# A fused attention, GRU and block-attention kernel: second attention's inverses in two tiles, residual begun with three outputs, recurrent weights split in the last batch, first batch by halves of the heads

## The chip, the cores and the metric

One core of a Trainium2 chip runs the whole program. The metric is device time in microseconds (us), the median of several executions. Beside it there is one profiled execution, from which every row below is taken. PE is TensorE (its weight loads are PEld), DVE is VectorE, ACT is ScalarE, POOL is GpSimd, and SP is the engine that issues most transfers.

## The reference

```python
x = x + L0(x, mask=cond)   # batch 8, 256 channels, 512 positions: 16 heads of 16, masked softmax attention
x = x + L1(x, emb=cond)    # 256 tokens of 512: FiLM scale/shift = cond @ W_emb + b_emb, RMS norm,
                           # qkv, RMS norm of each head, 16 heads of 32, softmax; returns o + o @ W_out
x = x + L2(cond, x)        # GRU over 256 steps: gi = x @ W_ih + b_ih, gh = h @ W_hh + b_hh
x = x + L3(x)              # 8 blocks of 32 tokens: keys, softmax over blocks, projection, layer norm
```

## The kernel before

The program has three blocks in sequence: `attention` (L0 and L1 of all 8 batches), `recurrence` (the GRU) and `block_attention`. Between two blocks all engines meet.

**Attention.** Each engine walks the same written-out lists of steps, so the lists are the order of the work. For batch b there are `ATTEND[b]` (32 score units of the first attention, `st`, and their weighting, `pv`) and `BESIDE[b]`. `BESIDE[b]` finishes the second attention of batch e = b-1 (`score1`, `weigh1`, `inv1`, `out1`, `res`, `xT`), computes queries and keys of batch b (`tokens`, `xnT`, `qk`), and puts between them the 32 `max` steps, in which PE computes scores of batch b+1 and DVE reduces them to maxima (L1034). `BESIDE[7]` has no maxima, since there is no ninth batch. `ALONE0` comes first: the 32 maxima of batch 0 with nothing beside them, `neg`, and `row`, a small transpose whose result ACT sends by a transfer into `q_rep`; the first scores wait for that. `LONE` comes last: the second attention of batch 7 alone.

**The end of the second attention of a batch.** Heads go in G = 4 groups. `weigh1` g writes weighted values and sums of group g into bank g % 2 of `bank_pair_D`. `inv1` g on ACT makes the inverse of the sums with Ln (L900) and Exp (L902) in one tile `inv_sum`. `out1` g on DVE multiplies it onto the values and writes quarter g of `oT` (L1068). `res` oc on PE (L737, L740), for each of four output chunks, adds the tokens by two products with the identity and then four products of `W_out` with the four quarters of `oT`. `xT` on DVE (L1027) ends the batch.

**The start.** PE computes the queries of batch 0 (L546, `bank_pair_A`), the keys (`bank_pair_B`), the values (L558) and the eight FiLM chunks of four products each (L782). ACT and DVE split queries and keys into high and low halves of f16 (`q_hi`, `q_lo`, `k_hi`, `k_lo` in `parts`); SP stores each of the four to DRAM (L464), waits for all, and loads them back spread over partitions for the four groups of heads (`load_rep`, L476). The maxima of a group wait for its load.

**The recurrence.** Its prologue splits `W_hh` and makes the input products of the first 32 steps, 12 chunks m of 16 products (L1233) in two banks in turn, which ACT moves out (L1373). `W_hh` is loaded (L1217) and then split by ACT (L1389) ahead of the moves of chunks 3 to 6, and by DVE (L1421). The last four chunks have transposes of `Wk` and `Wo` ahead of them (L1301). L1317 opens the banks of the first step, and 256 steps follow.

```python
                if g >= 1:
                    act.wait_ge(oT_ok, e * G + g)
                nc.scalar.activation(inv_sum[:, :], pD[:, g % 2, N:2 * N], ACT.Ln).then_inc(log1_ok, 1)
```

Of the kernel before, what the change touches and what calls it, by code (L numbers as in the profile page):

```python
# [10 lines left out]
ALU = mybir.AluOpType  # L11
# [3 lines left out]
P = 128  # L15
# [6 lines left out]
G = H // 4  # L22
# [18 lines left out]
def build(nc, x, cond, Wq0, Wk0, Wv0, b0, W_emb, b_emb, g_norm, W_qkv, g_q, g_k, W_out,  # L41
          W_ih, W_hh, b_ih, b_hh, rms_w, Wk3, Wo3, gamma, beta, out):
    top = ExitStack()
    with top:
# [6 lines left out]
        def scratch(name, shape, dt):  # L51
# [16 lines left out]
        w_ih = (w_in, sem("w_ih_ld"), sem("w_ih_hi"), sem("w_ih_lo"))  # L68

        attention(nc, sem, sb, x, cond, Wq0, Wk0, Wv0, b0, W_emb, b_emb, g_norm, W_qkv, g_q, g_k, W_out,  # L70
                  mask_rows, parts0, parts1, pA, pB, pC, pD, xT, ident, condT, rep, W_ih, w_ih)
# [7 lines left out]
        recurrence(nc, sem, sb, W_ih, W_hh, b_ih, b_hh, Wk3, Wo3, pA, pB, pC, pD, xT, ident, condT, rep, w_ih, woT, block_sums,  # L79
# [8 lines left out]

def key_weights(rep):

    start = DC * 3 * D
    return as_f32(rep)[:, start:start + DC * D].rearrange("p (c n) -> p c n", c=DC)


def attention(nc, sem, sb, x, cond, Wq0, Wk0, Wv0, b0, W_emb, b_emb, g_norm, W_qkv, g_q, g_k, W_out,
              mask_rows, parts0, parts1, pA, pB, pC, pD, xT, ident, condT, rep, W_ih, w_ih):

    w_in, w_ih_ld, w_ih_hi, w_ih_lo = w_ih
    with ExitStack() as ctx:
# [40 lines left out]

        hi1 = parts[:, 0:2, :, :].rearrange("p a c (e n) -> p a (c e) n", e=2)
# [6 lines left out]
        inv_sum = t("inv_sum", [P, N])  # L148
# [22 lines left out]
        with ExitStack() as prep:  # L171
# [66 lines left out]
            def _(pe):  # L238
# [9 lines left out]
                for c in range(DC):  # L248
# [16 lines left out]
                             "exp1_ok", "pv1_ps", "inv1_ok", "log1_ok", "oT_ok", "res_ps", "xT_ok"))  # L265
        ticked, log0_ok, x1_last, ld_rep1_end = (sem(n) for n in ("ticked", "log0_ok", "x1_last", "ld_rep1_end"))
# [49 lines left out]
        def finish_order(with_max):  # L316
# [85 lines left out]
        def lone_order():  # L402
# [23 lines left out]
        ALONE0 = [("max", u) for u in range(U0)] + [("neg", 0), ("row", 0)]  # L426
# [6 lines left out]
        def _(sp):  # L433
# [31 lines left out]

            def load_rep(b, g):
# [6 lines left out]
                sp.wait_ge(st_parts, b * 64 + 64)  # L473
# [33 lines left out]
            for b in range(B):  # L507
# [21 lines left out]
                spread1(b)  # L529

        @block.tensor
        def _(pe):
            def project_qk(b, which, n):
# [14 lines left out]
                if n == NC * NC - 1:  # L548
                    last.then_inc((q_ps, k_ps)[which], 1)
# [181 lines left out]
            def residual(e, oc):  # L731

                if oc == 0:
                    pe.wait_ge(oT_ok, e * G + G)
                o = pD[:, oc // 2, (oc % 2) * N:(oc % 2) * N + N]
                for tc in range(NC):
                    nc.tensor.matmul(o[:, tc * P:tc * P + P], x1[e % 2][:, tc, oc * P:oc * P + P], ident[:, :],  # L737
                                     start=(oc % 2 == 0 and tc == 0), stop=False, skip_group_check=True)
                for c in range(DC):
                    last = nc.tensor.matmul(o, wout[:, c, oc * P:oc * P + P], oT[:, c, :], start=False, stop=(c == DC - 1),  # L740
                                            skip_group_check=True)
# [3 lines left out]
            def steps(order, b, e):  # L745

                for kind, n in order:
# [10 lines left out]
                    elif kind == "max":  # L758
                        max_scores(b + 1, n)
                    elif kind == "row":  # L760
# [18 lines left out]
            def film_chunk(m):  # L779

                for k in range(DC):
# [4 lines left out]
            for which in range(2):  # L786
                for n in range(NC * NC):
                    project_qk(0, which, n)
# [3 lines left out]
            pe.wait_ge(c_emb, 32)  # L792
            for m in range(2 * DC):
                film_chunk(m)
# [10 lines left out]
        def _(act):  # L805
            def q_parts(b):

                act.wait_ge(q_ps, b + 1)
# [50 lines left out]
            def qk_chunk(e, m):  # L859
# [9 lines left out]
                def hi_part(m):  # L869
                    if m == 0 and e + 1 < B:  # L870
                        act.wait_ge(st_parts, e * 64 + 128)
# [964 lines left out]
```

## Time and profile before

| | us |
|---|---|
| median of 3 runs (1967.75 to 1971.98) | 1971.07 |
| the profiled execution | 1970.45 |
| span of its trace | 1968.5 |
| PE busy | 1854.3 (94%) |
| DVE busy | 1260.1 (64%) |
| ACT busy | 1090.5 (55%) |
| POOL busy | 378.4 (19%) |

In the rows further down a line of the timeline reads: start and duration in us, engine, source line, operation, output<-inputs, shape, the count of instructions merged, and in brackets the idle time ahead of it with what ended it. Ends of matmuls are modelled, and a full row of PE is not PE at its peak. PEclk is the granted clock of PE as a share of 2.4 GHz, so 0.50 is 1.2 GHz.

### The profile page before, as it was taken

The numbers are of one execution on the slowest core, as the hardware profiler recorded it, in microseconds if no ns is written. First come the engines' busy times: TensorE is split into PE (matmuls) and PEld (weight loads), VectorE is DVE, ScalarE is ACT, GpSimd is POOL, SyncE is SP. The second block draws the span as 40 slices with busy tenths as digits, with TensorE's granted clock in tenths as the row PEclk, the third lists the DMA queues.
The fourth block names the chain that finished last, engine by engine and source line by source line (L and its number), as shares of the span: only waits on it lengthen the run. The fifth ranks groups of instructions, "written<-read, shape, count | busy, mean of one in ns | idle before, by whom it ended". The sixth has DMA issues, their size and how long they took to land. (4 is left out here: it accounts for less than half of the span.)

```text
span 1968.5 us, 87065 instructions
## 1 busy us (share of the span) xinstructions
PE 1854.3 (94%) x33006; PEld 1408.4 (72%) x33006; DVE 1260.1 (64%) x5543; ACT 1090.5 (55%) x4105; POOL 378.4 (19%) x1398
## 2 busy tenths in 40 slices
PE   7877999999999999999978999999999999999996
PEld 4234465565646556464747999999999999999995
DVE  5545474746647475573244777777777777777767
ACT  0342737547373664737534665656565656666555
POOL 3000000000000000000001434343434343433335
PEclk7688999999999999999988999999999999999997
DMA  5221313233041322203223000000000000000002
GB/s 177 87 82 44 94 31 101 68 81 88 19 114 37 87 81 65 88 2 81 87 47 114 0 1 0 0 0 0 0 0 0 0 0 0 0 0 1 0 0 86
DMA packets 103525, 86.73 MB, mean 44 GB/s; under 512 B 15616, under 2 KB 90496, under 8 KB 103440
## 3 DMA queue, kind: packets, MB, share of 16 engines
q1 hardware_dynamic: 102416, 85.43, 15.3%
q8 instruction: 57, 0.93, 0.2%
q0 software_dynamic: 384, 0.01, 0.0%
q14 instruction: 28, 0.23, 0.0%
q10 hardware_dynamic: 640, 0.13, 0.0%
HBM read 60.20 MB, written 21.00 MB: 41 GB/s over the span
## 5 line engine op out<-in xcount | busy, mean ns | idle before, releaser
L1246 PE MATMUL bank_pair_A<-moving,rep 128*128 128x16 f16 x8192 | 317.9, 169 | 2.5 <-ACT bank_pair_C L1337 1.4
L1246 PE MATMUL bank_pair_B<-moving,rep 128*128 128x16 f16 x8192 | 315.4, 169 | 0.0
L1246 PE MATMUL bank_pair_C<-moving,rep 128*128 128x16 f16 x8192 | 315.4, 169 | 0.0
L1246 PEld LDWEIGHTS bank_pair_A<-moving,rep 128*128 128x128 f16 x8192 | 274.4, 96 | 14.3 <-issue 4.1
L1346 ACT ACTIVATE r_gate<-r_pre 128x16 f32<-128x16 f32 x512 | 110.5, 216 | 285.6 <-DVE r_pre L1437 285.6
L1246 PEld LDWEIGHTS bank_pair_B<-moving,rep 128*128 128x128 f16 x8192 | 258.9, 96 | 0.0
L1246 PEld LDWEIGHTS bank_pair_C<-moving,rep 128*128 128x128 f16 x8192 | 258.8, 96 | 0.0
L1233 PE MATMUL bank_pair_D<-x_part,w_in 128*128 128x256 f16 x1536 | 198.8, 275 | 7.0 <-ACT gi_rz L1373 4.4
L1034 DVE TENSOR_REDUCE head_max<-bank_pair_A 128x2 f32<-128x1024 f32 x128 | 155.9, 1218 | 56.6 <-PE bank_pair_A L579 56.4
L1437 DVE TENSOR_REDUCE r_pre<-bank_pair_A 128x16 f32<-128x32 f32 x512 | 97.9, 191 | 136.2 <-PE bank_pair_A L1246 136.2
L1128 POOL TENSOR_TENSOR x<-x,w_in 128x512 f32<-128x512 f32 x8 | 10.2, 1271 | 896.3 <-DMA w_in<-w_in 896.3
L1034 DVE TENSOR_REDUCE head_max<-bank_pair_B 128x2 f32<-128x1024 f32 x128 | 155.6, 1216 | 21.3 <-PE bank_pair_B L579 20.8
L1233 PEld LDWEIGHTS bank_pair_D<-x_part,w_in 128*128 (+1 forms) x1536 | 138.3, 98 | 23.4 <-ACT gi_rz L1373 4.7
L836 ACT ACTIVATE probs<-bank_pair_A 128x1024 f32<-128x1024 f32 x128 | 130.9, 1023 | 43.4 <-PE bank_pair_A L598 43.1
L1527 POOL COPY n_terms<-gi_n 128x32 f32 (+1 forms) x257 | 53.8, 209 | 487.5 <-DVE moving L1488 437.6
L610 PE MATMUL bank_pair_C<-probs,w_in 128*32 128x512 f32 x1024 | 136.9, 607 | 0.2 <-ACT probs L836 0.2
L836 ACT ACTIVATE probs<-bank_pair_B 128x1024 f32<-128x1024 f32 x128 | 131.1, 1024 | 7.7 <-PE bank_pair_B L598 7.7
L598 PEld LDWEIGHTS bank_pair_A<-rep 128*128 128x128 f16 x512 | 40.6, 98 | 115.9 <-ACT probs L836 95.5
L1346 ACT ACTIVATE z_gate<-z_pre 128x16 f32<-128x16 f32 x512 | 110.6, 216 | 20.2 <-DVE z_pre L1441 9.1
L1446 DVE TENSOR_TENSOR n_terms<-bank_pair_B,r_gate 128x32 f32<-128x32 f32 x512 | 97.7, 191 | 28.7
L879 ACT ACTIVATE sq<-bank_pair_C 128x256 f32<-128x256 f32 x48 | 18.4, 383 | 169.4 <-PE bank_pair_C L640 169.4
L1346 ACT ACTIVATE cand<-n_pre 128x16 f32<-128x16 f32 x512 | 107.0, 209 | 0.0
(262 smaller groups left out, 3764.0 us busy)
## 6 DMA issues: line engine op xcount, KB each, us to landing
rep<-parts SPq DMA_DIRECT2D x256, 64.0 KB
parts<-parts SPq DMA_DIRECT2D x48, 256.0 KB, 2.1
q_rep<-parts SPq DMA_DIRECT2D x32, 256.0 KB, 5.0
k_rep<-parts SPq DMA_DIRECT2D x64, 128.0 KB, 2.9
w_in<-in_x_dram SPq DMA_DIRECT2D x8, 512.0 KB, 3.9
x<-in_x_dram SPq DMA_DIRECT2D x8, 512.0 KB, 4.0
w_in<-w_in SPq DMA_DIRECT2D x128, 32.0 KB, 2.0
parts<-parts SPq DMA_DIRECT2D x32, 128.0 KB, 2.6
```

Source lines behind the costliest of these rows:

```text
L598: last = nc.tensor.matmul(pair[u % 2][:, j // 2, (j % 2) * N:(j % 2) * N + N], k_rep[:, h, kc * P:kc * P + P], q_rep[:, h, queries], start ...
L610: last = nc.tensor.matmul(pC[32 * j:32 * j + 32, g % 2, :], v_aug[:, kc, 4 * g + j, :], probs[w % 2][:, j, :], start=(kc == 0), stop=(kc = ...
L836: nc.scalar.activation(probs[u // 2 % 2][:, :, u % 2 * N:u % 2 * N + N], pair[u % 2][:, :, :].rearrange("p a (b t) -> p (a b) t", b=2), AC ...
L879: nc.scalar.activation(sq[m % 2][:, :], qk_bank[m % 3][:, 0:N], ACT.Square).then_inc(sq_ok, 1)
L1034: nc.vector.tensor_reduce(head_max[:, 2 * n:2 * n + 2], pair[n % 2][:, :, :], AX.X, ALU.max).then_inc(s_max, 1)
L1128: nc.gpsimd.tensor_tensor(x1[b % 2][:, c, :], x1[b % 2][:, c, :], y[:, c, :], ALU.add).then_inc(x1_ok, 1)
L1233: last = nc.tensor.matmul(bank, w_in[w][:, k, bass.ts(m, P)], x_part[:, part, k, :, :].rearrange("p b t -> p (b t)"), start=(k == 0 and w ...
L1246: last = nc.tensor.matmul(ps[part][:, o:o + 2 * B], w[:, k, (first + c) * P:(first + c) * P + P], moving[j % 2][:, k, :, :].rearrange("p s ...
L1346: nc.scalar.activation(dst[:, SLICE[part], :], src[:, SLICE[part], :], func, scale=1.0 / GS).then_inc(done, 1)
L1437: nc.vector.tensor_reduce(r_pre[:, SLICE[part], :], halves(pR[part]), AX.X, ALU.add).then_inc(r_sum, 1)
L1446: nc.vector.tensor_tensor(n_terms[:, SLICE[part], 0:2, :], pN[part].rearrange("p (c s b) -> p c s b", s=2, b=B), r_gate[:, SLICE[part], :] ...
L1527: nc.gpsimd.tensor_copy(n_terms[:, :, 2, :], gi_n[:, bass.ds(step, 1), :, :].rearrange("p o c b -> p (o c) b")).then_inc(n_in, 1)
```

## The change

It has four parts, all in `attention` and in the prologue of `recurrence`.

1. `inv_sum` becomes two tiles (those of `head_rstd`), so `inv1` of a group waits for the `out1` of two groups before. In `BESIDE` the `out1` of the third group moves ahead of `weigh1` of the fourth, and the `out1` of the fourth ahead of the second of two maxima.
2. `residual` starts once three quarters of `oT` are there: for chunks 0 and 1 it adds tokens and three products each, waits for the fourth quarter, then adds the fourth products of both. Chunks 2 and 3 are as before.
3. `W_hh` is loaded into the tile of `W_qkv` after the last use of it, and split in `LONE`, by ACT after its last inverse and by DVE between the last `out1` and `xT`. The load and split are gone from the recurrence.
4. In batch 0 queries and keys are computed, split and stored by halves of the heads: groups 0 and 1 are loaded after the first half is stored, groups 2 and 3 after the second. On DVE the addition of the bias to `q_rep` (L1079) goes between the halves. Of the eight FiLM chunks three stay ahead of the maxima, one goes ahead of `row`, four follow it.

```diff
@@ finish_order (BESIDE)
             yield "inv1", G - 2
+            yield "out1", G - 2
             yield "weigh1", G - 1
-            yield from maxes(1)
-            yield "out1", G - 2
             yield "inv1", G - 1
             yield from maxes(1)
             yield "out1", G - 1
+            yield from maxes(1)
             yield "tokens", 0
...
@@ lone_order and alone_order
             yield "out1", G - 1
+            yield "w_hh", 0
...
+            for m in range(3):
+                yield "film", m
+            for u in range(U0):
+                yield "max", u
+            yield "neg", 0
+            yield "film", 3
+            yield "row", 0
+            for m in range(4, 2 * DC):
+                yield "film", m
...
@@ SP
-            store_parts(0, 0)
-            store_parts(0, 1)
-            for g in range(G):
-                load_rep(0, g)
+            for c in range(2):
+                store_first(c)
+                for g in range(2 * c, 2 * c + 2):
+                    load_rep(0, g)
...
                 spread1(b)
+            sp.wait_ge(v1_ps, B)
+            sp.dma_start(wqkv[:, :, :], W_hh.rearrange("(c p) n -> p c n", p=P)).then_inc(w_ld, 16)
...
@@ residual on PE
                 if oc == 0:
+                    pe.wait_ge(oT_ok, e * G + (G - 1))
+                if oc < 2:
+                    tokens_part(oc)
+                    weights_part(oc, range(DC - 1))
+                if oc == 1:
                     pe.wait_ge(oT_ok, e * G + G)
+                    weights_part(0, (DC - 1,))
+                    weights_part(1, (DC - 1,))
+                if oc >= 2:
+                    tokens_part(oc)
+                    last = weights_part(oc, range(DC))
...
@@ inverse1 on ACT
-                if g >= 1:
-                    act.wait_ge(oT_ok, e * G + g)
-                nc.scalar.activation(inv_sum[:, :], pD[:, g % 2, N:2 * N], ACT.Ln).then_inc(log1_ok, 1)
+                if g >= 2:
+                    act.wait_ge(oT_ok, e * G + (g - 1))
+                nc.scalar.activation(inv_sum[g % 2][:, :], pD[:, g % 2, N:2 * N], ACT.Ln).then_inc(log1_ok, 1)
...
+            def split_w_hh():
+                act.wait_ge(w_ld, 16)
+                act.wait_ge(w_ih_lo, DC)
+                for k in range(DC):
+                    nc.scalar.activation(w_part[0][:, k, :], wqkv[:, k, :], ACT.Copy, scale=WS).then_inc(w_hi, 1)
...
@@ batch 0 on ACT
-            q_parts(0)
-            k_part(0)
+            for c in range(NC):
+                act.wait_ge(q_ps, c + 1)
+                nc.scalar.activation(q_hi[:, c, :], pA[:, c, :], ACT.Copy, scale=QS).then_inc((half_hi, q_hi_ok)[c], 1)
...
+                nc.scalar.activation(k_hi[:, c, :], kf[:, c, :], ACT.Copy).then_inc((half_hi, k_hi_ok)[c], 1)
...
@@ batch 0 on DVE
+            dve.wait_ge(ld_mask, 16)
+            for c in range(NC):
...
+                if c == 0:
+                    dve.wait_ge(c_b, 3)
+                    nc.vector.tensor_scalar(q_rep[64:67, :, :], q_rep[64:67, :, :], brow[64:67, 0:1], None, ALU.add).then_inc(c_b, 1)
...
@@ recurrence
-            sp.dma_start(staged, W_hh.rearrange("(c p) n -> p c n", p=P)).then_inc(w_ld, 16)
...
-                if W_HH_FROM <= m < W_HH_FROM + DC:
-                    k = m - W_HH_FROM
-                    if k == 0:
-                        act.wait_ge(w_ld, 16)
-                    nc.scalar.activation(w_part[0][:, k, :], staged[:, k, :], ACT.Copy, scale=WS).then_inc(w_hi, 1)
                 evacuate(0, m, pG[m % 2], m >= RZ)
```

The first place is PE between the last maximum of batch 0 and the first scores. `bank_pair_D<-condT,probs` are the FiLM products, `bank_pair_A<-ident,head_max` is `row`. Before:

```order
L579 MATMUL bank_pair_B<-rep 128x512 x2
L585 MATMUL bank_pair_A<-ident,head_max 64x128
L598 MATMUL bank_pair_A<-rep 128x256 x4
L598 MATMUL bank_pair_B<-rep 128x256 x4
L546 MATMUL bank_pair_D<-w_in,W0T 128x512
```

The same place with the change:

```order
L611 MATMUL bank_pair_B<-rep 128x512 x2
L835 MATMUL bank_pair_D<-condT,probs 128x8 x4
L617 MATMUL bank_pair_A<-ident,head_max 64x128
L835 MATMUL bank_pair_D<-condT,probs 128x8 x16
L630 MATMUL bank_pair_A<-rep 128x256 x4
L630 MATMUL bank_pair_B<-rep 128x256 x4
```

Five FiLM chunks, 20 products, now stand around `row`, 16 of them between it and the first scores; 12 of the 32 remain ahead of the maxima.

The second place is the end of the second attention of a batch with maxima, on DVE. The rows with `oT` are `out1`, those with `xnT` are the normed tokens. Before, from the `out1` of the second group:

```order
L1068 TENSOR_TENSOR oT<-bank_pair_D,inv_sum 128x256
L1034 TENSOR_REDUCE head_max<-bank_pair_B 128x2
L1034 TENSOR_REDUCE head_max<-bank_pair_A 128x2
L1068 TENSOR_TENSOR oT<-bank_pair_D,inv_sum 128x256
L1034 TENSOR_REDUCE head_max<-bank_pair_B 128x2
L1068 TENSOR_TENSOR oT<-bank_pair_D,inv_sum 128x256
L1001 TENSOR_SCALAR xnT<-bank_pair_C,film_scale,film_shift 128x256 x4
```

With the change:

```order
L1135 TENSOR_TENSOR oT<-bank_pair_D,head_rstd 128x256
L1099 TENSOR_REDUCE head_max<-bank_pair_B 128x2
L1135 TENSOR_TENSOR oT<-bank_pair_D,head_rstd 128x256
L1099 TENSOR_REDUCE head_max<-bank_pair_A 128x2
L1135 TENSOR_TENSOR oT<-bank_pair_D,head_rstd 128x256
L1099 TENSOR_REDUCE head_max<-bank_pair_B 128x2
L1066 TENSOR_SCALAR xnT<-bank_pair_C,film_scale,film_shift 128x256 x4
```

Each of the last two `out1` stands one maximum earlier.

The third place is ACT from the last inverse of the last batch to the moves of the recurrence's chunks (`gi_rz`). Before:

```order
L902 ACTIVATE inv_sum<-inv_sum 128x256
L99 UNCONDITIONAL_BRANCH
L1322 UNCONDITIONAL_BRANCH
L1326 ACTIVATE x_part<-xT 128x256 x4
L1327 ACT_TABLE_LOAD
L1373 ACTIVATE gi_rz<-bank_pair_D,bias_in 128x8x32 x3
L1389 ACTIVATE rep<-gi_rz 128x1536
L1373 ACTIVATE gi_rz<-bank_pair_D,bias_in 128x8x32
```

With the change:

```order
L953 ACTIVATE head_rstd<-head_rstd 128x256
L992 ACTIVATE rep<-wqkv 128x1536 x4
L107 UNCONDITIONAL_BRANCH
L1402 UNCONDITIONAL_BRANCH
L1406 ACTIVATE x_part<-xT 128x256 x4
L1407 ACT_TABLE_LOAD
L1453 ACTIVATE gi_rz<-bank_pair_D,bias_in 128x8x32 x8
```

The four splits of 1536 columns leave the moves and stand ahead of the boundary between the blocks.

## Rows read from the trace of the kernel before

**Rows 1.** Timeline of batch 0 up to the first maximum

```profile
15.05 0.19 PEld L546 LDWEIGHTS bank_pair_A<-w_in,W0T 128*128 128x128 f32 x1 [0.46 <-issue]
...
16.96 1.02 ACT L811 ACTIVATE parts<-bank_pair_A 128x1024 f16<-128x1024 f32 x1 [14.93 <-PE bank_pair_A L546]
...
20.47 1.29 DVE L962 SCALAR_TENSOR_TENSOR kf<-bank_pair_B,w_in 128x512 f32<-128x512 f32 x2 [1.23 <-PE bank_pair_B L546]
...
22.95 1.23 DVE L969 TENSOR_TENSOR parts<-kf,parts 128x1024 f16<-128x1024 f32 x1 [1.19 <-ACT parts L815]
...
23.65 9.12 PE L782 MATMUL bank_pair_D<-condT,probs 128*128 128x8 f32 x64
...
26.34 4.70 SPq L476 DMA_DIRECT2D rep<-parts  x8
...
33.85 1.22 DVE L1034 TENSOR_REDUCE head_max<-bank_pair_A 128x2 f32<-128x1024 f32 x1 [9.68 <-PE bank_pair_A L579]
```

**Rows 2.** Timeline from the last maximum of batch 0 to the first scores

```profile
70.49 1.22 DVE L1034 TENSOR_REDUCE head_max<-bank_pair_B 128x2 f32<-128x1024 f32 x1
...
72.00 0.69 PE L585 MATMUL bank_pair_A<-ident,head_max 128*64 128x128 f32 x2 [1.55 <-DVE head_max L1037]
...
75.25 1.01 PE L598 MATMUL bank_pair_A<-rep 128*128 128x256 f16 x4 [2.57 <-DMA rep<-max_row]
```

**Rows 3.** Windows: busy time (instructions) by engine, PEclk, DMA share, GB/s

```profile
26.00:29.00 3.00, 3.00 (x28) 3.00 (x27) 0.00 (x0) 0.00 (x0) 0.00 (x0) 0.94 0.13 37
29.00:32.80 3.80, 3.77 (x18) 3.70 (x19) 0.00 (x0) 0.00 (x0) 0.00 (x0) 0.50 0.45 134
...
79.00:80.00 1.00, 1.00 (x5) 0.69 (x3) 0.00 (x0) 0.29 (x1) 0.00 (x0) 0.58 0.00 0
```

**Rows 4.** Timeline of the end of a second attention, e = 0

```profile
269.80 0.42 ACT L902 ACTIVATE inv_sum<-inv_sum 128x256 f32<-128x256 f32 x1
...
271.62 1.23 DVE L1034 TENSOR_REDUCE head_max<-bank_pair_A 128x2 f32<-128x1024 f32 x1 [2.24 <-PE bank_pair_A L579]
...
272.76 0.41 DVE L1068 TENSOR_TENSOR oT<-bank_pair_D,inv_sum 128x256 f32<-128x256 f32 x1
...
273.27 0.38 ACT L900 ACTIVATE inv_sum<-bank_pair_D 128x256 f32<-128x256 f32 x1 [3.05 <-DVE oT L1068]
...
274.69 0.71 PE L737 MATMUL bank_pair_D<-ident,x 128*128 128x128 f32 x4 [1.80 <-DVE oT L1068]
```

**Rows 5.** Waits of all attention from 85 us: total us, times, longest

```profile
PE bank_pair_D L737 <- DVE oT L1068: 12.6, 8, 1.8
```

**Rows 6.** Windows, the stage behind the residual of e = 0

```profile
286.00:312.00 26.00, 26.00 (x109) 18.72 (x108) 17.66 (x27) 13.02 (x33) 0.00 (x0) 1.00 0.30 63
```

**Rows 7.** Timeline of the last batch

```profile
984.99 5.59 ACT L939 ACTIVATE w_in<-rep 128x1536 f16<-128x1536 f32 x4
...
1004.28 6.75 DVE L1102 SCALAR_TENSOR_TENSOR w_in<-rep,w_in 128x1536 f16<-128x1536 f32 x4
...
1022.95 0.71 PE L737 MATMUL bank_pair_D<-ident,x 128*128 128x128 f32 x4 [1.41 <-DVE oT L1068]
...
1031.95 1.23 DVE L1027 TENSOR_TENSOR xT<-bank_pair_D,oT 128x1024 f32<-128x1024 f32 x1 [9.05 <-PE bank_pair_D L740]
```

**Rows 8.** Timeline of the recurrence's prologue

```profile
1034.50 10.56 PE L1233 MATMUL bank_pair_D<-x_part,w_in 128*128 128x256 f16 x80 [2.59 <-DVE x_part L1403]
...
1047.35 1.48 ACT L1389 ACTIVATE rep<-gi_rz 128x1536 f16<-128x1536 f32 x1 [5.05 <-DMA gi_rz<-in_L_cond_W_hh_dram]
...
1049.48 6.93 PE L1233 MATMUL bank_pair_D<-x_part,w_in 128*128 128x256 f16 x48 [4.42 <-ACT gi_rz L1373]
...
1056.25 1.04 PE L1301 MATMUL bank_pair_A<-ident,gi_rz 128*128 128x128 f32 x8
```

**Rows 9.** Windows of the prologue

```profile
1040.00:1045.00 5.00, 5.00 (x47) 4.29 (x44) 0.00 (x0) 1.26 (x2) 0.00 (x0) 1.00 1.02 422
```

**Rows 10.** A transfer of the prologue: KB, us from issue to landing

```profile
gi_rz<-in_L_cond_Wk_dram SPq DMA_DIRECT2D x1, 1024.0 KB, 14.3
```

More of the change, by code:

```diff
@@ L78, in build @@
         norm_from = (cond, rms_w, beta, gamma)
-        recurrence(nc, sem, sb, W_ih, W_hh, b_ih, b_hh, Wk3, Wo3, pA, pB, pC, pD, xT, ident, condT, rep, w_ih, woT, block_sums,
+        recurrence(nc, sem, sb, b_ih, b_hh, Wk3, Wo3, pA, pB, pC, pD, xT, ident, condT, rep, w_ih, w_hh, woT, block_sums,
                    norm, norm_from)
@@ L86, in as_f32, with halves_of_weights @@
     return rep[:, :, :, :].rearrange("p n h d -> p (n h d)").bitcast(F32)
+def halves_of_weights(rep):
+    words = rep[:, :, :, :].rearrange("p n h d -> p (n h d)")[:, 0:2 * DC * 3 * D].rearrange("p (s c n) -> p s c n", s=2, c=DC)
+    return [words[:, n, :, :] for n in range(2)]
 def key_weights(rep):
@@ L265, in attention @@
                              "exp1_ok", "pv1_ps", "inv1_ok", "log1_ok", "oT_ok", "res_ps", "xT_ok"))
+        half_hi, half_low = (sem("half_" + n) for n in ("hi", "low"))
         ticked, log0_ok, x1_last, ld_rep1_end = (sem(n) for n in ("ticked", "log0_ok", "x1_last", "ld_rep1_end"))
@@ L424, in lone_order, with alone_order @@
             yield "xT", 0
-        ALONE0 = [("max", u) for u in range(U0)] + [("neg", 0), ("row", 0)]
+        def alone_order():
+            for m in range(3):
[7 more added lines that the diff above has]
+                yield "film", m
+        ALONE0 = list(alone_order())
         ATTEND = [list(attend_order(b)) for b in range(B)]
@@ L731, in residual, with tokens_part, out_of, weights_part @@
             def residual(e, oc):
-                if oc == 0:
-                    pe.wait_ge(oT_ok, e * G + G)
[L735 to L741, printed above, removed]
+                def tokens_part(oc):
+                    for tc in range(NC):
+                        nc.tensor.matmul(out_of(oc)[:, tc * P:tc * P + P], x1[e % 2][:, tc, oc * P:oc * P + P], ident[:, :],
+                                         start=(oc % 2 == 0 and tc == 0), stop=False, skip_group_check=True)
+                def out_of(oc):
+                    return pD[:, oc // 2, (oc % 2) * N:(oc % 2) * N + N]
+                def weights_part(oc, chunks):
+                    for c in chunks:
+                        last = nc.tensor.matmul(out_of(oc), wout[:, c, oc * P:oc * P + P], oT[:, c, :], start=False, stop=(c == DC - 1),
+                                                skip_group_check=True)
+                    return last
+                if oc == 0:
+                    pe.wait_ge(oT_ok, e * G + (G - 1))
[3 more added lines that the diff above has]
+                if oc == 1:
+                    pe.wait_ge(oT_ok, e * G + G)
+                    weights_part(0, (DC - 1,))
[3 more added lines that the diff above has]
+                    last = weights_part(oc, range(DC))
                 if oc == DC - 1:
@@ L1097, in _, with split_w_hh @@
             nc.vector.tensor_scalar(gk[:, :], gk[:, :], QS * DH1 ** 0.5, None, ALU.mult).then_inc(c_gains, 1)
+            def split_w_hh():
+                for k in range(DC):
+                    dve.wait_ge(w_hi, k + 1)
+                    nc.vector.scalar_tensor_tensor(out=w_part[1][:, k, :], in0=wqkv[:, k, :], scalar=WS, in1=w_part[0][:, k, :],
+                                                   op0=ALU.mult, op1=ALU.subtract).then_inc(w_lo, 1)
             def split_w_ih():
@@ L1188, in recurrence @@
         RZ = 2 * DC
-        W_HH_FROM = 3
         def halves(ps):
```

81 lines of the change are left out of this document (50 added, 31 removed).

## Prediction

> **What bounds the kernel now.** I read the table of busy times first: TensorE (PE) is at 94% of the span, so the attention blocks and the recurrence are rows of PE work with gaps, and a gap that is closed shortens the program if PE stays busy after it. So I went through the waits of PE, then the timeline around each gap that the change touches, then the windows for the clock. The reader should see four things.
> First, the start. PE is idle or slow for 72 us. The split keys of batch 0 end on DVE at 22.95 + 1.23 = 24.18, the loads of group 0 go out from 26.34, and the first maximum is reduced at 33.85 [rows 1]. From there DVE alone sets the pace: 32 maxima from 33.85 to 70.49 + 1.22 = 71.71 [rows 1, 2], or 1.18 each.
> Second, PE waits for `out1` at the head of the residual: 12.6 us in 8 batches [rows 5], 1.80 in a batch with maxima [rows 4] and 1.41 in the last [rows 7]. Six such batches make 10.8, so batch e = 6 has 12.6 - 10.8 - 1.41 = 0.4.
> Third, after it PE is busy without a gap (26.00 of 26.00 us) [rows 6].
> Fourth, the recurrence's prologue. Five chunks of products end at 1034.50 + 10.56 = 1045.06, then PE stands 4.42 us, because the move of a bank is queued on ACT behind the split of `W_hh`, and that waited 5.05 us for its load; three more chunks then take 6.93, and the first transposes start at 1056.25 [rows 8].
>
> **Part 4, the halves.** Moved, not added: the same bytes in eight stores of half the size, with a second wait for stores. The fifth weight load of the queries starts at 15.05 [rows 1]; the four ahead of it are the first half of the heads for both chunks of channels, so ACT can take `q_hi` of the first half at 15.1. Half of 1.02 is 0.5, with a fixed share some 0.6: 15.7. DVE needs 1.29 / 2 = 0.65: `q_lo` to 16.4. The second products end near 16.9, since the first full bank was read at 16.96 [rows 1]. `kf` 0.65 to 17.6, `k_hi` on ACT 0.6 to 18.2, `k_lo` 0.65 to 18.9. The whole keys end at 24.18 now, 5.3 later. Behind that the chain is unchanged: 2.16 from `k_lo` to the loads (24.18 to 26.34) puts them at 21.1, and the first maxima at most 5.3 earlier. In PE nothing is in the way: 24 of the 64 FiLM instructions remain ahead, 2.6 us at 0.107 each (28 in 3.00) [rows 3], which end at 23.65 + 2.6 = 26.3, before the loads land. The bias (L1079) now stands between the halves on DVE; the second half of the stores is issued behind 16 loads on SP near 30, and groups 2 and 3 land by about 41, while their maxima are due 16 times 1.18 behind 28.5, at 47. So the second half costs nothing; the cover is 6 us. Value: -5.3.
> **Part 4, the FiLM chunks.** The 40 instructions taken from the front return at the end of the maxima, where the clock is half. FiLM ran there at 0.107 each at full clock and 0.211 at half (18 in 3.80) [rows 3]. Chunk 3, 8 instructions, takes 1.7 in a gap of 1.55 ahead of `row` [rows 2]: +0.15. The 32 behind `row` take 6.75 us at half clock. `row` ends near 72.6, so they end at 79.5 in the old times, where the scores began at 75.25 after a transfer [rows 2]. That transfer hides 2.6 us of them. What is queued behind them is the first scores, and for those ACT waits. So +4.1. Start in all: -5.3 + 0.15 + 4.1 = -1.1.
> The clock decides that term. It read 1.00 after dense products, fell from full to half while PE was busy with FiLM products alone (0.94 on average in 26 to 29, 0.50 in 29 to 32.8) [rows 3], and came back in 79 to 80, some 4.3 us after the scores began at 75.25 [rows 2, 3]. I therefore take FiLM as work that doesn't raise it. By the Trainium skill (TensorE: Matmul & The Clock Gate, Part 1) activity of PE releases the throttle; by that rule PE, busy from chunk 3 on, would have its full clock before the scores. This trace speaks against counting FiLM as such activity, but shows only the fall, not the rise; it is the second rival.
>
> **Parts 1 and 2, six batches with maxima.** Now: Exp of group 2 ends at 270.22, DVE is idle 2.24 us before a maximum at 271.62, `out1` of group 2 comes behind it at 272.76, the Ln of group 3 at 273.27 waited 3.05 for that, and PE starts the residual at 274.69 [rows 4]. With the change `out1` of group 2 falls into DVE's idle time at 270.3. Ln and Exp of group 3 need only PE's sums, which end ahead of the products of the maximum reduced at 271.62; with 0.38 + 0.42 they are done by 272.4. Its `out1` takes the old place at 272.76 and ends at 273.2. PE, free at 274.69 - 1.80 = 272.89, needs three quarters only, so it goes on at once, and has 3.5 us of products before it needs the fourth (a chunk of the residual is a quarter of 1031.95 - 1022.95 [rows 7], 2.25, and all but the fourth products of two chunks come first). The gap goes whole: 1.80 each, -10.8. DVE's second maximum keeps its place, and the maxima inside the residual stay a step ahead of PE. After it PE shows no idle time in 26 us [rows 6], and what it releases (loads, `qk`, `xT`) hangs on it and shifts along.
> **Batch e = 6 and the last.** 0.4 and 1.41 [rows 5, 7]: PE fills them with products of three quarters. In the last batch DVE now has four splits of `W_hh` ahead of `xT`. On ACT they take 5.59 / 4 = 1.40 each and can start at 1022.45, on DVE 6.75 / 4 = 1.69 each [rows 7]: from 1023.9 to 1030.7. The residual would end at 1031.95 - 1.41 = 1030.5, so `xT` loses 0.1 to 0.2. Together -0.4 - 1.3 = -1.7. The load of 3 MB is issued behind the last spread of keys near 996 and has 26 us to land; in the prologue today the same load ends ACT's wait at 1047.35 [rows 8], issued at the block's start near 1034.5, so under 13 us. Nothing stands behind it on SP.
>
> **Part 3, the prologue.** Without split and wait the moves keep ahead of PE, as they did in the first five chunks, which ran without a gap [rows 8]. At full clock a product takes 5.00 / 47 = 0.106 [rows 9], a chunk of 16 takes 1.70. The last three before the transposes then end at 1045.0 + 5.1 = 1050.1, not 1056.25: -6.1. Some of that is clock, since PE also came back slow after the gap. The transposes need `Wk` and `Wo`. `Wk` took 14.3 us with 3 MB ahead of it [rows 10]; now it is issued where those were, at the start of the block near 1034.5, and even 14.3 would give 1049, before PE asks. `Wo`, of the same size, follows it. Value: -6.0.
>
> **The sum.** -1.1 - 10.8 - 1.7 - 6.0 = -19.6. The profiled execution took 1970.45, its span being 1968.5, so 1950.8; the median is 0.6 above it, so 1951.4. I forecast 1951. What follows, 256 steps and the block attention, is unchanged.
>
> **Rivals.**
> 1. The halves bring nothing: DVE's order or the landing of the smaller stores holds the first maxima where they are. For it: 2.16 us from `k_lo` to the loads is a wait for landing, paid twice now. Against: PE's 5.3 are on the chain. Then the start costs +4.2 instead of -1.1, time 1956.5. Chance 0.12.
> 2. FiLM counts as activity. The clock rises about 4.3 us after chunk 3 starts, at 74.8; by then some 10 of the 32 instructions have run, the other 22 take 2.4, and the scores start at 77.2 at full clock. Today they start at 75.25 and lose 2.2 at half clock, which is 77.4. The +4.1 vanishes: 1947. Chance 0.15.
> 3. The freed PE time is not passed on in the six batches: DVE, with its maxima, or a transfer ends the next wait. For it: DVE is 18 of 26 us busy there. Against: no idle time of PE after the residual [rows 6]. Half lost gives 1956.5, all lost 1962. Chance 0.1.
> 4. Slower. The half clock after the maxima persists into the first `ATTEND`, because PE meets it with long FiLM work of low load instead of a pause. Each microsecond of dense work at half clock costs 0.5, so it decides from 39 us more at half clock on; with 60, 1981. For it: PE stayed at half clock through the maxima. Against: the same scores raised it in 4.3 us [rows 2, 3]. Chance 0.02.
> The forecast itself (1949 to 1954) has 0.58; the rest are small mixtures around it.
>
> **Range and chances.** It must reach rival 2 below and rivals 1 and 3 in part above: 1946 to 1958. A measurement of this kernel tells 0.2%, 4 us. Only rival 4 and an unforeseen wait of that size end above 1967: faster 0.95, same 0.03, slower 0.02.
>
> **What would show it.** After: the first maximum on DVE near 28.5; FiLM products behind `row` for 6 to 7 us at half clock, and the first scores 1 us earlier than now; no wait of PE at the head of any residual; `xT` of the last batch right behind four splits on DVE; no gap of PE in the prologue, and the first transposes of `Wk` some 20 us before 1056.25. I am wrong if scores start before 72 or after 76, if PE's idle time at the residual returns a few steps later, or if the last maxima of keys wait longer for their load.

## The result, and the profile after

The changed kernel took 1946.35 us (median of 4 runs, 1945.18 to 1949.10) beside 1969.41 for the kernel before: a ratio of 0.9879, 95% interval 0.9862 to 0.9895. The same kernel in another set of runs gave 0.9869 (0.9854 to 0.9885). The mean of the two ratios, 0.9874, is 24.8 us less than the 1970.4 of before; the forecast's sum was 19.6. Wherever a gain or loss in us is given below, it is a difference of such ratios times 1970.4. The profiled execution took 1949.1 us and is the slowest of its four, its span 1947.1.

The page's table of busy times of the changed kernel:

```profile
PE 1852.5 (95%) x33006; PEld 1410.3 (72%) x33006; DVE 1262.5 (65%) x5545; ACT 1092.0 (56%) x4107; POOL 379.4 (19%) x1398
```

PE's busy time is 1.8 us below that of before, the span 21.4: the time came out of PE's idle time.

**The start.** Timeline of the changed kernel up to the first maximum, the place of [rows 1]:

```profile
11.54 1.95 PE L578 MATMUL bank_pair_A<-w_in,W0T 128*128 128x512 f32 x4 [1.82 <-PEq L179]
...
13.53 0.60 ACT L1002 ACTIVATE parts<-bank_pair_A 128x512 f16<-128x512 f32 x1 [11.49 <-PE bank_pair_A L578]
...
15.13 0.69 DVE L1148 SCALAR_TENSOR_TENSOR parts<-bank_pair_A,parts 128x512 f16<-128x512 f32 x1 [3.07 <-DMA w_in<-in_cond_dram]
...
17.11 0.69 DVE L1157 TENSOR_TENSOR parts<-kf,parts 128x512 f16<-128x512 f32 x1 [0.69 <-ACT parts L1007]
...
19.54 3.62 SPq L506 DMA_DIRECT2D rep<-parts  x8
...
21.93 2.74 PE L835 MATMUL bank_pair_D<-condT,probs 128*128 128x8 f32 x24
...
26.05 0.60 PE L611 MATMUL bank_pair_A<-rep 96*128 96x512 f16 x2 [1.38 <-DMA rep<-parts]
...
26.69 1.23 DVE L1099 TENSOR_REDUCE head_max<-bank_pair_A 128x2 f32<-128x1024 f32 x1 [3.73 <-PE bank_pair_A L611]
```

`q_hi` of the first half starts at 13.53. `q_lo` could follow at 14.13, but DVE waited for the load of the mask until 15.13, a wait that the forecast doesn't have. `k_lo` ends at 17.80, the loads go out at 19.54 and the first maximum is reduced at 26.69 instead of 33.85. The forecast said 28.5; experiment 9 shows why this execution was earlier still. PE now waits 1.38 us for the load, where it came from FiLM without a pause before.

From the last maxima to the first scores, the place of [rows 2], and two windows of the clock, one behind the first maxima and one behind the first scores (PEclk is the third number from the end):

```profile
63.08 1.71 PE L835 MATMUL bank_pair_D<-condT,probs 128*128 128x8 f32 x8
...
64.59 0.20 DVE L1102 TENSOR_SCALAR head_max<-head_max 128x64 f32<-128x64 f32 x1
64.84 0.69 PE L617 MATMUL bank_pair_A<-ident,head_max 128*64 128x128 f32 x2
65.45 7.00 PE L835 MATMUL bank_pair_D<-condT,probs 128*128 128x8 f32 x32
...
72.30 1.01 PE L630 MATMUL bank_pair_A<-rep 128*128 128x256 f16 x4
```

```profile
27.00:30.00 3.00, 2.13 (x5) 0.26 (x4) 3.00 (x3) 0.00 (x0) 0.00 (x0) 0.50 0.72 232
78.00:79.00 1.00, 1.00 (x6) 0.59 (x5) 0.00 (x0) 0.22 (x1) 0.00 (x0) 0.98 0.08 16
```

The 32 instructions take 7.00 us, 0.219 each, which is the half clock throughout. From `row` to the scores it is 7.46 us, before 3.25 [rows 2]. The clock is at its full level from about 78, 5.7 us behind the first scores.

**The end of a second attention.** Timeline of the changed kernel, e = 0, the place of [rows 4]:

```profile
268.41 0.42 DVE L1135 TENSOR_TENSOR oT<-bank_pair_D,head_rstd 128x256 f32<-128x256 f32 x1 [0.86 <-ACT head_rstd L953]
...
269.27 0.38 ACT L951 ACTIVATE head_rstd<-bank_pair_D 128x256 f32<-128x256 f32 x1 [0.89 <-PE bank_pair_D L758]
...
270.01 1.04 PE L655 MATMUL bank_pair_C<-ident,xn 128*128 128x128 f32 x8
...
270.89 0.61 PE L767 MATMUL bank_pair_D<-ident,x 128*128 128x128 f32 x4
270.92 0.41 DVE L1135 TENSOR_TENSOR oT<-bank_pair_D,head_rstd 128x256 f32<-128x256 f32 x1
```

The residual follows the transposes of the tokens with no idle time, and the fourth `out1` ends at 271.33, while PE still works on three quarters. The first products take 0.61 us where they took 0.71 behind the wait [rows 4]. PE's waits from 200 to 1060 us (total, times, longest) have no line of the residual left, where there were 12.6 us [rows 5]; the two largest that are left there are these:

```profile
PE bank_pair_A L707 <- DMA k_rep<-parts: 7.9, 2, 6.2
PE bank_pair_D L715 <- DVE head_max L1132: 7.3, 8, 2.0
```

**The last batch and the prologue**, the places of [rows 7] and [rows 8]:

```profile
1006.02 5.59 ACT L992 ACTIVATE rep<-wqkv 128x1536 f16<-128x1536 f32 x4
...
1007.52 6.76 DVE L1180 SCALAR_TENSOR_TENSOR rep<-wqkv,rep 128x1536 f16<-128x1536 f32 x4 [0.95 <-ACT rep L992]
...
1014.20 1.22 DVE L1092 TENSOR_TENSOR xT<-bank_pair_D,oT 128x1024 f32<-128x1024 f32 x1
...
1016.74 15.77 PE L1313 MATMUL bank_pair_D<-x_part,w_in 128*128 128x256 f16 x128 [2.64 <-DVE x_part L1478]
...
1032.35 1.04 PE L1381 MATMUL bank_pair_A<-ident,gi_rz 128*128 128x128 f32 x8
```

The splits lie beside PE's residual and `xT` follows them at 1014.20. The eight chunks ahead of the transposes run through in 15.77 us without a gap; from their start to the transposes it is 15.61, before 21.75 [rows 8].

How far the changed kernel is ahead of before in the two profiled executions: first scores 2.95; first residual 3.81; start of the last batch's residual 17.81; prologue 17.76; transposes 23.90; end 21.4. The recurrence gives none of this back: from the transposes to the first products of the block attention (1032.35 to 1891.83, before 1056.25 to 1915.79) it is 859.5 us in both traces. The 2.5 us are given back in the block attention, which the change doesn't touch: 55.3 us from there to the end, before 52.7. Its length differs between traces (52.8 in experiments 10 and 11, 53.8 in 4 and 7, 55.2 in 9 and 12); what makes the difference stays open.

### The profile page after: what moved, and what is told of

It is laid out like the page before. It is cut to its first block and busy times, and to the rows that moved or that the text cites. A ratio compares the mean times of both kernels' runs of the same rounds, so it can differ in the third digit from the quotient of the medians.

```text
span 1947.1 us, 87066 instructions
## 1 busy us (share of the span) xinstructions
PE 1852.5 (95%) x33006; PEld 1410.3 (72%) x33006; DVE 1262.5 (65%) x5545; ACT 1092.0 (56%) x4107; POOL 379.4 (19%) x1398
## 5 line engine op out<-in xcount | busy, mean ns | idle before, releaser
L1212 POOL TENSOR_TENSOR x<-x,w_in 128x512 f32<-128x512 f32 x8 | 10.2, 1272 | 878.6 <-DMA w_in<-w_in 878.6
```

## The experiments

The ratios are to the kernel before, with 95% intervals. A part is undone when it alone is taken out of the changed kernel, and what that loses is read against 0.9874, the mean of the changed kernel's two ratios. A part is alone when nothing else of the change is made to the kernel before. The intervals are about 3 us to either side, so a loss of 1 or 2 us is not told from none.

**1. Part 4 undone** (halves and FiLM as before).

```diff
-            for m in range(3):
+            for m in range(8):
                 yield "film", m
...
-            for c in range(2):
-                store_first(c)
-                for g in range(2 * c, 2 * c + 2):
-                    load_rep(0, g)
+            store_parts(0, 0)
+            store_parts(0, 1)
+            for g in range(G):
+                load_rep(0, g)
```

> The changed kernel with batch 0 as it was: queries and keys split and stored whole, eight FiLM chunks ahead of the maxima. Theory A (the terms of the sum are right, and the 3 us more than forecast are where PE's clock happened to be low in single executions): the first scores start 1 to 3 us later than with the change, the loss of 1.8 seen in the profile's start being half clock (the full clock came at 9.8 us there and at 15.0 before); time 1.1 to 3 above the changed kernel, 1947.5 to 1949.5. Theory B (the start was worth 1.1 + 3.5): 4.6 above, 1951.

1947.93 us, 0.9881 (0.9865 to 0.9896): 1.4 us lost. That is theory A's size, though the interval doesn't exclude B's 4.6; experiment 7 narrows it.

**2. Part 3 undone** (`W_hh` loaded and split in the recurrence).

```diff
-            yield "w_hh", 0
...
+                if 3 <= m < 3 + DC:
+                    k = m - 3
+                    if k == 0:
+                        act.wait_ge(w_ld, 16)
+                    nc.scalar.activation(w_part[0][:, k, :], staged[:, k, :], ACT.Copy, scale=WS).then_inc(w_hi, 1)
                 evacuate(0, m, pG[m % 2], m >= RZ)
```

> The changed kernel with the load and split of W_hh back in the recurrence's prologue. Theory A: 6.0 of the prologue comes back, less 0.15 that xT loses behind the splits: 5.9 above the changed kernel, 1952.2. Theory B (the last batch pays for the load and the splits, as its longer stretch at half clock in the profile may say): 4 above or less, 1950.3, and the last batch of this run is faster than with the change.

1952.41 us, 0.9902 (0.9887 to 0.9916): 5.5 us lost, near A. From the prologue's first product to the transposes it is 20.84 us in its trace. B asked for a faster last batch. From the seventh residual to the eighth it takes 67.36 us here and 68.28 in the changed kernel, but with 10.2 us at half clock against 17.1; experiment 1, which has part 3 and also 10.2 us at half clock, takes 66.50. So the traces don't show that the load and the splits cost the last batch anything.

**3. Parts 1 and 2 undone.**

```diff
+            yield from maxes(1)
+            yield "out1", G - 2
             yield "inv1", G - 1
...
                 if oc == 0:
-                    pe.wait_ge(oT_ok, e * G + (G - 1))
...
+                    pe.wait_ge(oT_ok, e * G + G)
+                tokens_part(oc)
+                last = weights_part(oc, range(DC))
```

> The changed kernel with one tile of inverses, the old order of out1 and the old residual. Theory A: 10.8 + 0.4 + 1.4 = 12.6 above the changed kernel, 1959. Theory B (the gaps were worth more, since closing them also keeps the clock up or frees DVE): 15 to 16 above, 1962. PE waits again 12.6 us at the head of the residuals.

1960.75 us, 0.9944 (0.9928 to 0.9960): 13.8 us lost. A and B both lie in the interval; the time doesn't choose between them.

**4. Five FiLM chunks ahead, one before `row`, two behind.**

```diff
-            for m in range(3):
+            for m in range(5):
...
-            for m in range(4, 2 * DC):
+            for m in range(6, 2 * DC):
```

> The changed kernel with five FiLM chunks ahead of the maxima, one ahead of row and two behind it, instead of 3, 1 and 4. In the changed kernel's profile PE stands 1.38 us ahead of the first maximum, and a chunk takes 0.9 there at full clock and 1.75 behind row. Theory A: two more chunks ahead delay the first maximum by 0.4 us and take 3.5 from behind row, of which 0.1 is below the transfer: scores 3 us earlier, 1943.3. Rival: the maxima wait for more, or the clock falls during the five chunks (it fell at 26.85 in the changed kernel's profile): no gain, 1946 to 1947.

1944.13 us, 0.9867 (0.9850 to 0.9885). The direction is A's, but 1.4 us are not told apart by these intervals. In the trace the scores follow the last maximum's `neg` by 4.30 us, against 7.71 in the changed kernel.

**5. Part 1 alone undone** (the first hunk of 3, and one tile of inverses).

```diff
-        inv_sum = head_rstd
+        inv_sum = [head_rstd[0], head_rstd[0]]
...
-                if g >= 2:
-                    act.wait_ge(oT_ok, e * G + (g - 1))
+                if g >= 1:
+                    act.wait_ge(oT_ok, e * G + g)
```

> Only part 1 is undone (one tile of inverses, the old order of inv1, weigh1 and out1 of the last two groups); the residual still begins with three quarters. Theory A, the early residual carries the gain nearly alone: in the old order the third quarter was ready at 272.76 + 0.41 = 273.17 and PE was free at 272.89, so PE waits 0.3 us at the head of the residual in six batches, 1.8 us in all, and never for the fourth quarter, which is needed 3.5 us later. That gives 1948.2 us, a ratio to before of 0.989. Rival B, the two parts bring half of the 1.9 us each: 6 us are lost, 1952.5, ratio 0.991. Rival C, undoing part 1 costs nothing at all: 1946.4.

1951.98 us, 0.9901 (0.9884 to 0.9918): 5.3 us lost, so B by the time. The trace has the wait that A named, and nothing of B's half a gap. Waits of PE, and the residual's head in the timeline:

```profile
PE bank_pair_D L767 <- DVE oT L1135: 2.0, 6, 0.3
```

```profile
272.95 0.71 PE L767 MATMUL bank_pair_D<-ident,x 128*128 128x128 f32 x4 [0.34 <-DVE oT L1135]
```

But 0.34 of wait lengthened that batch's stretch from ACT's move of `row` to the residual by 0.50 (78.76 against 78.26). Up to the seventh residual the trace is 3.8 us longer than those of the kernels with both parts (the table further down: 0.50 and 669.87 against 666.61), which is twice A's 1.8. How far the 5.3 are more than that, the interval leaves open.

**6. Part 2 alone undone** (the second hunk of 3).

```diff
                 if oc == 0:
-                    pe.wait_ge(oT_ok, e * G + (G - 1))
+                    pe.wait_ge(oT_ok, e * G + G)
```

> Only part 2 is undone: the residual waits for all four quarters at its head; the two tiles of inverses and the moved out1 stay. Theory A: in the trace of the changed kernel PE is free for the residual at 270.78 and the fourth out1 ends at 270.92 + 0.41 = 271.33, so PE waits some 0.6 us in six batches, 3.4 us; to this come the 0.4 of the seventh batch and up to 1.4 of the last, where no maximum stood in the way before: 5 us lost, 1951.4, ratio 0.9908. Rival B, part 1 alone closes the gap: 1947 at most. Rival C, part 1 alone closes nothing because the out1 stays behind a maximum: 13 us lost, 1959.

1952.58 us, 0.9906 (0.9889 to 0.9922): 6.3 us lost, A. The waits:

```profile
PE bank_pair_D L767 <- DVE oT L1127: 3.8, 8, 1.4
```

Each part undone loses 5 to 6 us, both together 13.8 (experiment 3), so either alone brings more than half: each gives `oT` more time, and they overlap.

**7. Part 4 alone on before** (edits 2 and 3 together).

```diff
-            yield "w_hh", 0
...
-                    pe.wait_ge(oT_ok, e * G + (G - 1))
+                    pe.wait_ge(oT_ok, e * G + G)
```

> Part 4 alone on the kernel before; parts 1, 2 and 3 undone. The trace of the changed kernel has the first scores 2.95 us earlier than before, the row of batch 1 1.85 us earlier; with part 4 undone that row was 0.7 us earlier. Theory A, part 4 is worth 1 to 2 us in time: ratio to before 0.999 (0.998 to 1.0). Rival B, the forecast's other ends: halves bring nothing, +4 us, ratio 1.002; or 5.3 us gained without a cost of FiLM, ratio 0.997.

1969.61 us, 0.9993 (0.9984 to 1.0002): 1.4 us gained, 3.2 at most, and the interval just includes nothing. A. The row of the residual's wait is back at 12.6 us, 8 times.

**8. All FiLM chunks ahead, halves kept.**

```diff
-            for m in range(3):
+            for m in range(8):
                 yield "film", m
...
-            yield "film", 3
             yield "row", 0
-            for m in range(4, 2 * DC):
-                yield "film", m
```

> The changed kernel with all eight FiLM chunks ahead of the maxima, as before, and the halves of the heads kept. Theory A, halves and FiLM trade one against the other as forecast: 40 instructions at 0.107 delay the first maximum by 4.3 less the 1.4 us in which PE waited for the load, to 29.6, and the scores follow row and its transfer only, near 71.0 to 71.5 instead of 72.3. So 1 us faster than the changed kernel, ratio 0.9874. Rival B: FiLM ahead costs more, because the first products then run at half clock: ratio 0.9889, 2 us slower.

1948.11 us, 0.9871 (0.9855 to 0.9886): the same time as the changed kernel, and A's ratio. A's mechanism was wrong all the same: its first maximum at 29.6 came at 36.88. This trace is of an execution 5 us above the kernel's median (1953.24), whose clock rose only at 17.6. Timeline of this kernel, then two windows:

```profile
24.97 11.00 PE L834 MATMUL bank_pair_D<-condT,probs 128*128 128x8 f32 x64
...
36.88 1.23 DVE L1098 TENSOR_REDUCE head_max<-bank_pair_A 128x2 f32<-128x1024 f32 x1 [11.42 <-PE bank_pair_A L610]
```

```profile
25.00:27.80 2.80, 2.80 (x28) 2.80 (x26) 0.46 (x1) 1.02 (x1) 0.00 (x0) 1.00 0.43 139
28.00:35.80 7.80, 7.80 (x38) 7.80 (x38) 0.00 (x0) 0.00 (x0) 0.00 (x0) 0.50 0.44 136
```

The clock fell while PE ran FiLM alone: 28 instructions in 2.80 us, then 38 in 7.80. So the last chunks cost half clock ahead of the maxima as well as behind them, and with all of them ahead PE, not the load, sets the first maximum: 36.88, against 37.17 in experiment 11, which has no halves and the same late start. [rows 1] has it already: FiLM ends at 23.65 + 9.12 = 32.77, and in the same trace the products of the first maximum start at 32.81, without a wait for the load. So by the traces the halves move the first maximum only because FiLM is moved. The times can't show it: 0.9871 here and 0.9881 without the halves (experiment 1) are not told apart.

**9. The changed kernel again** (no edit).

> The changed kernel again, unedited, beside the three below on one chip. Its first ratio was 0.9879 (0.9862 to 0.9895), 23.8 us below before, 4.2 more than the forecast's sum of 19.6. Theory A, the sum was short in its sizes (a fit over the kernels run so far gives 2.3 for part 4, 15.7 for parts 1 and 2 and 7.4 for part 3, 25.4 in all): 0.987 to 0.988 again. Theory B, the sum was right and the first ratio a lucky draw: 0.990.

1947.86 us, 0.9869 (0.9854 to 0.9885): A, above the forecast's 19.6 again. Its start in the timeline:

```profile
11.64 3.41 PE L578 MATMUL bank_pair_A<-w_in,W0T 128*128 128x512 f32 x4 [1.82 <-PEq L179]
...
28.32 1.23 DVE L1099 TENSOR_REDUCE head_max<-bank_pair_A 128x2 f32<-128x1024 f32 x1 [4.35 <-PE bank_pair_A L611]
```

The same four instructions took 1.95 us in the first trace. The clock rose in the one case before 10 us and in the other at 14.6, as it did at 15.0 in the trace of before. With that, the loads go out at 21.07 and the first maximum is at 28.32, where 21.1 and 28.5 were forecast.

**10. Part 3 alone on before** (edits 1 and 3 together).

```diff
+                    pe.wait_ge(oT_ok, e * G + G)
+                tokens_part(oc)
+                last = weights_part(oc, range(DC))
...
+            store_parts(0, 0)
+            store_parts(0, 1)
```

> Part 3 alone on the kernel before: W_hh loaded and split in the last batch, everything else as before. Theory A, the forecast's size: the gap of 4.42 us and the slow products after it go, 6.0 less, ratio 0.9969. Theory B, it is worth more (9.7 us between the kernel with parts 3 and 4 and the one with part 4 alone; 7.4 in the fit): 0.9950 to 0.9962. Rival C, less (4.5 us between the kernel with part 3 undone and the changed one): 0.9977.

1964.77 us, 0.9961 (0.9946 to 0.9976): 7.7 us gained; B's size, A within the interval. The prologue's stretch is 14.69 us in its trace.

**11. Parts 1 and 2 alone on before** (edits 1 and 2 together).

```diff
-            yield "w_hh", 0
...
+            store_parts(0, 0)
+            store_parts(0, 1)
```

> Parts 1 and 2 alone on the kernel before. Theory A, the waits at the head of the residual are all that goes: 10.8 + 1.7 = 12.5 us, ratio 0.9937. Theory B, a gap costs more than PE's listed wait, since the first product after it takes 0.71 instead of 0.61 and its weight load is in the open; the traces show 2.0 a batch and 14.4 us up to the seventh residual: 15.7 us, ratio 0.9920. Rival C, part of it is given back where no other part helps: 10 us, 0.9949.

1955.80 us, 0.9913 (0.9899 to 0.9928): 17.1 us gained. B (15.7); A's 0.9937 is outside the interval.

**12. FiLM among the maxima.** Two chunks as eight single products, one behind each fourth maximum; one chunk before `row`, two behind.

```diff
             for u in range(U0):
                 yield "max", u
+                if u % 4 == 3:
+                    yield "film1", 3 * DC + u // 4
             yield "neg", 0
-            yield "film", 3
+            yield "film", 5
             yield "row", 0
-            for m in range(4, 2 * DC):
+            for m in range(6, 2 * DC):
```

> The changed kernel with two FiLM chunks, eight products, spread one product behind every fourth maximum of batch 0, one chunk ahead of row and two behind it instead of four. Theory: DVE paces the maxima at 1.18 us, and PE has about 0.15 us of slack in each (20.89 busy of 24.00), 0.6 in four, against 0.44 for a product of two instructions at half clock. So the maxima end as before, 16 instructions behind row end 3.5 us earlier, and the first scores start near 69.0 instead of 72.3: 1943.0, ratio 0.986. Rival: a product behind a maximum delays the next fill of a bank by its whole 0.44, and DVE with it: 8 times 0.44 minus the slack, up to 3.5 us later, which cancels the gain: 1946.4.

1941.65 us, 0.9855 (0.9839 to 0.9871): the fastest kernel here, 3.7 us below the mean of the changed one, though the intervals overlap. It is as much as was expected, 3.5. Timeline:

```profile
30.59 1.23 DVE L1108 TENSOR_REDUCE head_max<-bank_pair_A 128x2 f32<-128x1024 f32 x1
...
31.48 0.43 PE L843 MATMUL bank_pair_D<-condT,probs 128*128 128x8 f32 x2
31.73 1.22 DVE L1108 TENSOR_REDUCE head_max<-bank_pair_B 128x2 f32<-128x1024 f32 x1
...
66.13 0.19 DVE L1111 TENSOR_SCALAR head_max<-head_max 128x64 f32<-128x64 f32 x1
...
70.75 1.01 PE L632 MATMUL bank_pair_A<-rep 128*128 128x256 f16 x4
```

From the first maximum (28.24) to `neg` it is 37.89 us, in the changed kernel 26.69 to 64.59, 37.90: the products fit into PE's slack at no cost to DVE. The scores follow `neg` by 4.62 instead of 7.71. So the expected mechanism is in the trace; only that it shortens the time is not beyond the intervals.

**All together.** A least-squares fit of three terms to eight of the ratios (the changed kernel twice, each of the three parts undone, each alone), weighted by their intervals:

| | forecast | alone on before | undone | fit |
|---|---|---|---|---|
| part 4 | 1.1 | 1.4 | 1.4 | 1.8 +- 1.4 |
| parts 1 and 2 | 12.5 | 17.1 | 13.8 | 16.5 +- 1.7 |
| part 3 | 6.0 | 7.7 | 5.5 | 7.4 +- 1.8 |
| all | 19.6 | | 24.8 | 25.7 |

The +- come from the runs' intervals alone; kernels measured together share the runs of before, so they are rather too small. By the fit part 4 can't be told from nothing, and parts 1 and 2 together are 4 us above their forecast, more than twice their +-.

## Why the prediction was right and where it fell short

The direction and the mechanisms held and none of the four rivals took their place. The size was 5.2 us short, 19.6 for 24.8, and by the traces about 3 of it are in one term, the six batches.

**Bounds.** Right. PE's gaps that were closed shortened the program whole, and by more than their length.

**Halves, -5.3.** Right for an execution whose clock rises as late as before's: 33.85 to 28.32 is 5.5 (experiment 9). The loads go out at 21.07 there, for 21.1. In the first trace the early clock made it 19.54, although DVE waited for the mask. The cover of the second half held. Rival 1 is refuted with FiLM where the change puts it. With FiLM ahead the halves bring nothing to the first maximum (experiment 8), though for another reason than the rival's: PE is busy.

**FiLM, +0.15 and +4.1.** Right: 7.00 us at half clock for 6.75 forecast, and 4.21 more between `row` and the scores. The chunk before `row` cost nothing (`neg` to `row` is 0.25 us in both). The clock rose 5.7 us behind the scores and never in FiLM, so rival 2 is refuted. By the Trainium skill (TensorE: Matmul & The Clock Gate, Part 1) activity releases the throttle; these traces show 7.00 us of back-to-back products of 8 columns that didn't release it, and 7.80 us at half clock in experiment 8. The start in all, -1.1, was -1.4 by experiments 1 and 7, which both leave room for it.

**Six batches, -10.8.** The mechanism was right and the term was mis-sized. The step that failed is "The gap goes whole: 1.80 each, -10.8": the gap did go, but I took the idle time of PE's row as its whole cost. In the traces a gap costs 2.07, which makes 12.4 for six, and with two effects that the forecast doesn't have the six batches lost 13.9. Stretches in the traces, in us, between starts:

| kernel | ACT's move of batch 1's `row` to first residual | first to seventh residual | of it at half clock |
|---|---|---|---|
| before | 80.22 | 680.52 | 6.83 |
| experiment 7 | 80.22 | 678.44 | 0 |
| experiment 10 | 80.22 | 679.00 | 3.41 |
| experiment 3 | 80.22 | 678.85 | 3.41 |
| experiment 5 | 78.76 | 669.87 | 0 |
| experiment 6 | 78.76 | 671.61 | 0 |
| the changed kernel | 78.26 | 665.97 | 0 |
| experiments 1, 2, 4, 8, 9, 11, 12 | 78.25 to 78.26 | 665.35 to 667.87 | 0 |

The first column: a wait of 1.80 costs 1.96, one of 0.34 costs 0.50. The 0.16 more is an overlap that a wait takes away. Without one the residual starts at 270.89, while the last transposes still run to 270.01 + 1.04 = 271.05; with one (timeline of before) they end at 271.85 + 1.04 = 272.89, and the wait of 1.80 counts from there. Behind the start comes another 0.11: from the first product of the residual to the first of `W_out` it is 0.44 without the wait and 0.55 (274.69 to 275.24) behind it. The first weight load stands behind the wait too: it starts together with the product at 274.69, where without a wait it starts 0.11 ahead of it (270.78). So a gap costs 1.80 + 0.16 + 0.11 = 2.07. From residual to residual, experiment 7 and the changed kernel differ by 2.00, 2.05 and 2.10 in three of five batches.

The second column has 12.6 between the mean of its first four rows (679.20) and the mean of the eight kernels with both parts (666.61), where the forecast has 5 x 1.8 + 0.4 = 9.4. Five gaps at 2.07 are 10.35, and the stretch to the seventh residual is 0.65 shorter than in experiment 7; together 11.0. Of the other 1.6 about 1.0 is the clock (below; 6.83 us of half clock made 2.1 between before and experiment 7, and the four kernels have 3.4 on average). About 0.6 is left. Between experiment 7 and the changed kernel, which both have no half clock there, 1.5 is left, in the two batches that differ by 2.51 and 3.16; whether the change does that or chance stays open. So the six batches are 1.96 + 12.6 - 0.65 = 13.9 by the traces, for 10.8 forecast.

**e = 6 and the last, -1.7.** 0.65, and 1.07 from the seventh residual to the last (69.35 in experiment 7, 68.28 in the changed kernel, both with 17.07 us at half clock): 1.7. `xT` waited for the splits no more than forecast: it starts 9.06 behind the last residual, before 9.00 [rows 7].

**Prologue, -6.0.** By the trace right: 21.75 to 15.61 where 3.4 us at half clock remain, 14.69 and 14.85 in two traces where none do (experiments 10 and 3), so 6.1 to 7.1. In experiments 2 and 11, which have the split in the prologue as before, it is 20.84 and 21.11, so one pair of traces can say anything from 5.2 to 7.1. The times, 5.5 undone and 7.7 alone, and the fit's 7.4 don't contradict the forecast.

**Rival 3**, the freed time not passed on, is refuted, **rival 4** too: the clock came back 5.7 us behind the first scores. The range, 1946 to 1958, held the measured 1946.35 by 0.35 us. The mean of the two ratios would put it at 1945.6, just outside, so that it was held is luck as much as judgement.

## What to carry to other kernels

Price a wait of PE by how far the work behind it shifts, not by the idle time in PE's row: here 1.80 us of idle time cost 2.07, and more where the clock fell behind it. When work is moved to clear the start, ask at which clock it runs in the new place, and look first for slack in a loop that another engine paces: in experiment 12 it cost that loop nothing. A part that is worth 0.1% alone can't be sized by one pair of kernels; undo it and do it alone, and fit.

## What the runs showed that I had not expected

**Short falls of the clock behind PE's gaps.** Windows of before, around the residual of e = 2, whose first product starts at 506.15 behind a wait of 1.80:

```profile
500.00:506.15 6.15, 4.35 (x60) 2.50 (x52) 3.91 (x6) 1.60 (x4) 0.00 (x0) 1.00 0.00 0
...
506.50:509.90 3.40, 3.40 (x12) 2.77 (x11) 1.41 (x4) 0.00 (x0) 0.00 (x0) 0.50 0.00 0
```

The same in experiment 3 at e = 1 (first product 388.72) and in experiment 10 at e = 3 (first product 623.50):

```profile
383.00:388.70 5.70, 3.91 (x52) 2.23 (x44) 3.46 (x6) 1.60 (x4) 0.00 (x0) 1.00 0.00 0
388.82:392.20 3.38, 3.38 (x10) 2.87 (x11) 1.65 (x4) 0.00 (x0) 0.00 (x0) 0.50 0.00 0
```

```profile
618.00:623.59 5.59, 3.79 (x49) 2.20 (x41) 3.35 (x6) 1.60 (x4) 0.00 (x0) 1.00 0.01 3
623.59:627.00 3.41, 3.41 (x10) 2.89 (x11) 1.66 (x4) 0.00 (x0) 0.00 (x0) 0.50 0.00 0
```

PE was busy for about 70% of the stretch ahead, the wait being part of it, and at half clock right behind. A fourth fall, in before at 899.0, stands behind waits of 1.32 and 0.68 us at the scores. The four kernels with the long gap have four such falls between the first and the seventh residual, the ten without it none. That is one trace each, and 21 of the 24 gaps in these four traces had no fall behind them, so it is a link and no rule. The Trainium skill (TensorE: Matmul & The Clock Gate, Part 1) has idle time bring the throttle back. The three falls behind a gap go that way, the 21 other gaps show that 1.80 us of it mostly didn't.

**When the clock rises at the start** differs between executions of one kernel: before 10 us and at 14.6 here (1.95 against 3.41 us for the same four instructions), 17.6 in experiments 8 and 11. It moves the first maximum by 1.6 us between the two traces of the changed kernel, as much as part 4 is worth.
